# Second norm's scale and shift on z's turned tiles instead of on w1, with fewer counting matmuls, another border and a last tile in halves

## The reference, cut to what matters

```python
xn = _layernorm(x, axis=-1)                       # x is 1250 x 1024
x = x + _L0_gnn_ref(xn, ...) + _L0_mix_ref(xn)    # 20000 edges, attention over them
x = x + _L0_ffn_ref(_layernorm(x))                # gate, up, down with rounded operands

def _L0_gnn_ref(x, W, a, src, dst):
    h = x @ W
    e = exp(-leaky_relu((h @ a_l)[src] + (h @ a_r)[dst], 0.1))
    rowsum = segment_sum(e, src, N)
    return elu(segment_sum(e[:, None] * h[dst], src, N) / (rowsum[:, None] + EPS))

def _L0_mix_ref(x, ...):
    x2 = _layer_norm(x, ln1_g, ln1_b)
    ...                                           # linear attention, cos and sin features
    x = x + (attn @ wo + bo)
    x2 = _layer_norm(x, ln2_g, ln2_b)             # the second norm, g2 and b2
    h = relu(x2 @ w1 + b1)                        # w1 is 1024 x 512
    return x + (h @ w2 + b2)
```

## Time and profile before

| | us |
|---|---|
| runs | 1209.41, 1206.21, 1209.04 |
| median of the runs | 1209.04 |
| the profiled execution, its own time | 1210.66 |
| its span | 1208.4 |
| PE busy | 1154.3 |
| DVE busy | 744.5 |
| ACT busy | 705.4 |
| POOL busy | 326.6 |

### The profile page before, as it was taken

The page is one execution under the profiler, slowest core; times in us unless marked ns, Lnnn a source line. Parts: engine busy times, 40 slices in busy tenths (PEclk is TensorE's granted clock), DMA queues, the critical chain, the costliest instruction groups (busy, mean ns, idle before and its releaser), DMA issues. The chain is left out here.

```text
span 1208.4 us, 19464 instructions
## 1 busy us (share of the span) xinstructions
PE 1154.3 (96%) x6733; PEld 1015.9 (84%) x6733; DVE 744.5 (62%) x1289; ACT 705.4 (58%) x1080; POOL 326.6 (27%) x295
## 2 busy tenths in 40 slices
PE   5999899999999999999899999999989999999997
PEld 2456699999999999999878778999968888887784
DVE  7888636656565565656774777777763222655656
ACT  8497267778777878777875433233344432554553
POOL 1300033333332324232122110666624331211100
PEclk9999999999999999999999999999997999999999
DMA  8000130202020202020537568233353323512103
GB/s 228 16 27 27 39 88 2 73 0 73 0 73 0 73 0 73 0 73 0 195 122 229 152 187 217 54 86 90 79 190 102 103 69 124 187 34 69 35 2 101
DMA packets 73736, 99.43 MB, mean 82 GB/s; under 512 B 27532, under 2 KB 54956, under 8 KB 73172
## 3 DMA queue, kind: packets, MB, share of 16 engines
q1 hardware_dynamic: 70224, 86.11, 25.3%
q0 software_dynamic: 3456, 12.58, 3.5%
HBM read 77.04 MB, written 21.63 MB: 82 GB/s over the span
## 5 line engine op out<-in xcount | busy, mean ns | idle before, releaser
L1149 POOL TENSOR_TENSOR cos_sin_lo<-cos_sin,cos_sin_hi 125x1024 fp32r<-125x1024 f32 (+1 forms) x40 | 95.6, 2391 | 225.3 <-ACT cos_sin_hi L1261 225.3
L1652 PE MATMUL rows_in_psum<-x,mix_hi_q 128*128 128x416 f32 (+1 forms) x384 | 104.0, 352 | 0.0
L1652 PE MATMUL rows_in_psum<-x,mix_hi_k 128*128 128x416 f32 (+1 forms) x376 | 102.8, 355 | 0.0
L850 PE MATMUL rows_in_psum<-h_hi,a_lo 125*125 125x342 f32 x300 | 96.4, 321 | 5.3 <-POOL a_lo L686 3.0
L1756 PE MATMUL rows_in_psum<-x,xt_hi 128*125 128x512 f32 x320 | 100.4, 395 | 0.0
L561 PE MATMUL rows_in_psum<-hot_s,hot_k 125*125 125x314 bf16 x396 | 87.5, 323 | 9.4 <-DVE hot_k L470 8.6
L850 PE MATMUL rows_in_psum<-h_lo,a_hi 125*125 125x342 f32 x300 | 95.7, 319 | 0.0
L850 PE MATMUL rows_in_psum<-h_hi,a_hi 125*125 125x342 f32 x300 | 95.7, 319 | 0.0
L1652 PE MATMUL rows_in_psum<-x,mix_hi_v 128*128 128x416 f32 (+1 forms) x336 | 91.3, 353 | 0.0
L1261 ACT ACTIVATE cos_sin_hi<-cos_sin 125x1024 fp32r<-125x1024 f32 (+1 forms) x80 | 83.6, 1045 | 7.3 <-PE rows_in_psum L1734 5.5
L561 PEld LDWEIGHTS rows_in_psum<-hot_s,hot_k 125*125 125x125 bf16 x396 | 41.5, 137 | 53.5 <-DVE hot_k L470 53.3
(11 more groups left out here) (342 smaller groups left out, 3115.4 us busy)
## 6 DMA issues: line engine op xcount, KB each, us to landing
x_in<-in_x_dram SPq DMA_DIRECT2D x31, 448.0 KB
attn_dram<-attn_t SPq DMA_DIRECT2D x8, 625.0 KB, 4.0
at_in<-attn_dram SPq DMA_DIRECT2D x10, 500.0 KB, 4.6
x_in<-gnn_dram SPq DMA_DIRECT2D x10, 448.0 KB
out_dram<-rows SPq DMA_DIRECT2D x10, 448.0 KB
mix_in_v<-in_L_mix_wv_dram SPq DMA_DIRECT2D x8, 512.0 KB, 6.1
mix_in_k<-in_L_mix_wk_dram SPq DMA_DIRECT2D x8, 512.0 KB, 4.8
mix_in_q<-in_L_mix_wq_dram SPq DMA_DIRECT2D x8, 512.0 KB, 6.9
```

The source lines that it names most:

```text
L850: last = pe.matmul(p_o[0:T, i % 2, n, 0:H_COLS], stationary(left, i, d), right[:, d, cols], start=(d == 0 and m == 0), stop=(d == NT - 1 a ...
L1149: pool.tensor_tensor(full(cs_lo, k), full(cs, k), f32(full(cs_hi, k)), ALU.subtract).then_inc(s_cslo[0], 1)
L1652: last = pe.matmul(p_w[:, n, 0:w], left[which][:, k, :], right[:, k, a:a + w], start=(k == 0 and m == 0), stop=(k == K8 - 1 and m == 2))
```

## The change

Five edits come together.

- Counting: the matmuls of zeros that opened a window are gone; the first chunk's matmuls start the banks instead, and the last chunk's end the first bank. One closing matmul of 2 columns is left. The first chunk stands ahead of the loop and the last two behind it, on PE and on VectorE.
- Border: SP's store of gnn tile 8 and its load of x(0) move from the end of the attention to the start of the project stage, in the other order, ahead of bo; the last addition of b2 moves from GpSimd to VectorE.
- Project stage: the 32 products of b2 with w1, and VectorE's addition behind them, are gone; w1 is split unscaled. z0's and z1's turned tiles are scaled and shifted by ScalarE out of PSUM, in eight pieces, and then copied.
- Feed forward: the same for z2 to z9 in keep_zt. The transposes wait for the scaled copy (s_zt), not for the lower half; normalise(i) waits for the lower half.
- Last tile: result(9) and its store come in two halves of 512 columns; PE signals s_d after each half of down(9). keep_hidden(8), ScalarE's copy of the turned hidden tile 8, waits for down(6) and no longer for down(7).

```diff
@@ counting, PE (VectorE likewise)
-                    for n, (a, w) in enumerate(BANK_PIECES):
-                        pe.matmul(p_cnt[0:T, t % TURNS, n, 0:w], zeros[:], zero_rows[:, 0:w], start=True, stop=False)
...
+                    def chunk(count, slot, start=False, stop=False):
+                        pe.wait_ge(s_hot, count)
+                        for n, (a, w) in enumerate(BANK_PIECES):
+                            last = pe.matmul(p_cnt[0:T, t % TURNS, n, 0:w], hot_k[:, slot, 0:T], hot_s[:, slot, a:a + w], start=start,
+                                             stop=(stop and n == 0))
+                        last.then_inc(s_used, 1)
...
+                    chunk(pe.snap(done, min_val=0, max_val=DONE_MOST) + 1, 0, start=True)
+                    with pe.Fori(first + HOT, past, HOT):
+                        before = pe.snap(done, min_val=0, max_val=DONE_MOST)
                         for j in range(HOT):
...
+                            chunk(before + j + 2, (j + 1) % HOT)
                         pe.reg_add(done, done, HOT)
-                    for n, (a, w) in enumerate(BANK_PIECES):
-                        last = pe.matmul(p_cnt[0:T, t % TURNS, n, 0:w], zeros[:], zero_rows[:, 0:w], start=False, stop=True)
-                    last.then_inc(s_tile, 1)
+                    before = pe.snap(done, min_val=0, max_val=DONE_MOST)
+                    for j in range(1, HOT):
+                        chunk(before + j + 1, j, stop=(j == HOT - 1))
+                    pe.reg_add(done, done, HOT)
+                    pe.matmul(p_cnt[0:T, t % TURNS, 1, 0:2], zeros[:], zero_rows[:, 0:2], start=False, stop=True).then_inc(s_tile, 1)
@@ border
-                if i < NT - 1:
+                if i < NT - 2:
                     store(i)
                     core.load_x(sp, (i + 2) % NT, i % 2)
...
-            add_b2(NT - 1)
-            pool.wait_ge(s_xb, NT)
+            pool.wait_ge(s_xb, NT - 1)
...
+            core.wait_x(dve, NT - 1, 1)
+            dve.tensor_tensor(x_in[:, 1, :], x_in[:, 1, :], b2[:], ALU.add).then_inc(s_xb, 1)
...
+            core.load_x(sp, 0, 0)
+            core.move(sp, core.gnn_dram[NT - 2], core.attended[:, 0, :], core.gnn_stored[0])
             core.move(sp, bo, spread(inp["L0_mix_bo"], T), s_bo)
@@ project stage
-                act.activation(core.w1_hi[:, k, :], w1_raw(k), ACT.Copy, scale=g2[:, k:k + 1]).then_inc(s_whi, 1)
+                act.activation(core.w1_hi[:, k, :], w1_raw(k), ACT.Copy).then_inc(s_whi, 1)
...
-                dve.scalar_tensor_tensor(core.w1_lo[:, k, :], w1_raw(k), g2[:, k:k + 1], f32(core.w1_hi[:, k, :]), ALU.mult,
-                                         ALU.subtract).then_inc(s_wlo, 1)
+                dve.tensor_tensor(core.w1_lo[:, k, :], w1_raw(k), f32(core.w1_hi[:, k, :]), ALU.subtract).then_inc(s_wlo, 1)
...
-            for f in range(F4):
-                for k in range(K8):
-                    last = pe.matmul(p_c[:, f:f + 1], w1_raw(k)[:, f * 128:(f + 1) * 128], b2c[:, k:k + 1], start=(k == 0),
-                                     stop=(k == K8 - 1))
-            last.then_inc(s_c, 1)
@@ feed forward, keep_zt on ScalarE
                 act.wait_ge(s_t, i + 1 - KEPT)
+                for k in range(K8):
+                    last = act.activation(zt(i)[:, k, :], p_t[:, k // 4, (k % 4) * T:(k % 4 + 1) * T], ACT.Identity,
+                                          scale=g2[:, k:k + 1], bias=b2c[:, k:k + 1])
+                last.then_inc(s_zt, 1)
                 act.wait_ge(s_1, F4 * (i // 2))
...
+                act.activation(zt_hi[:, :, (i % 2) * T:(i % 2 + 1) * T], zt(i), ACT.Copy).then_inc(s_thi, 1)
...
-                act.activation(hid[:, f, :], p_1[:, f % 2, 0:2 * T], ACT.Relu, bias=core.c1[:, f:f + 1]).then_inc(s_h, 1)
+                act.activation(hid[:, f, :], p_1[:, f % 2, 0:2 * T], ACT.Relu, bias=b1c[:, f:f + 1]).then_inc(s_h, 1)
...
-                    act.wait_ge(s_d, 2 * (i // 2))
...
+                    act.wait_ge(s_d, i - 1 if i >= NT - 2 else 2 * (i // 2))
...
-                pe.wait_ge(s_tlo, min(NT, 2 * (i // 2) + 6) - KEPT)
+                pe.wait_ge(s_zt, min(NT, 2 * (i // 2) + 6) - KEPT)
@@ last tile, PE and VectorE
+                    if n == 1 or i == NT - 1:
+                        last.then_inc(s_d, 1)
...
+            for n in range(2):
+                dve.wait_ge(s_d, NT + n)
+                half = rows[:, NT - 1, n * 512:(n + 1) * 512]
+                dve.scalar_tensor_tensor(half, down_at(NT - 1)[0:T, n, :], factor[:, NT - 1, 2:3], half, ALU.mult, ALU.add).then_inc(s_out, 1)
```

98 lines of the change are left out of this document (50 added, 48 removed).

## The result

The changed kernel takes 1211.31 us in the median of 19 runs (1210.02 to 1212.85), the kernel before 1209.04 us (19 runs, 1206.21 to 1211.31). The ratio is 1.0023 (95% interval 1.0017 to 1.0030): a little slower, 0.2%. The profiled execution took 1211.54 us, its span 1209.5.

What follows compares the result with a forecast made beforehand. PE was taken as the bound, busy 1154.3 of 1208.4 us. The terms -4.3 - 4.0 + 11.9 - 2.3 = +1.3 on a median of 1209.04 gave 1210.3 us, with an 8-in-10 range of 1204.2 to 1215.6.

Steps and rivals of the forecast that it cites:

- Same: Whole kernel: a time between 1205.4 and 1212.7 us, within 0.3% of the kernel before; chance 0.52.
- Counting: Counting stage: 80 zero matmuls removed and 20 short ones added save 4.3 us, ends 2.5 and 6.
- windows 2 to 11 gain next to nothing: Counting: ScalarE sets the pace in the ten windows that also carry the second norm, so they hardly gain.
- rival B: Counting: windows thought ScalarE-paced are paced by PE, gain 8.8 instead of 4.3 us, total 1205.8; chance 0.08.
- 0.41 for each of windows 12 to 19: Counting: each of these eight windows gains 0.27 us plus half of the closing pair, 3.3 in sum.
- low end: Counting: gain of only 2.5 us if the peeled loop's added branches take it back in eight windows.
- Border and products: Attention's end and project stage: shorter border and dropped w1 products together save 4.0 us, ends 2.5 and 6.
- Feed forward: Feed forward: eight activations in keep_zt make results late and PE wait, costing 11.9 us, ends 7 and 14.
- rival C: Feed forward: TensorE's clock falls in each of rounds 1 to 3, 4.5 us on top, total 1214.8; chance 0.15.
- Last tile: Tail: 1.1 us from PE's wait, 0.5 from VectorE's half, 0.7 from the smaller store, 2.3 us saved.
- Rival D: Project stage: products(2) starts no earlier, gains shrink from 4.0 to 1.0 us, total 1213.3; chance 0.14.
- A: Feed forward: delays overlap and a round waits once, costing 7 instead of 11.9 us, total 1205.4; chance 0.12.

Runs made afterwards that it cites:

- e_add_on_dve: Kernel before with one edit: the last addition of b2 runs on VectorE behind its last sum, not on GpSimd; 1207.59 us, ratio 0.9993.
- e_counts_closing: Kernel before with one edit: a counting window's two closing matmuls have 2 columns instead of 314 and 311; 1205.80 us, ratio 0.9979.
- e_ff_no_scale: Changed kernel with the feed forward's keep_zt as before, leaving out scale and shift of tiles 2 to 9; 1199.22 us, ratio 0.9927.
- e_ff_one_scale: Changed kernel with one activation of 1000 columns for the eight of 125 in the feed forward's keep_zt, values partly wrong; 1199.19 us, ratio 0.9919.
- e_ff_round_x_later: Changed kernel with keep_zt(2c+3) ahead of round_x(2c-1) in ScalarE's order of the feed forward; 1206.72 us, ratio 0.9988.
- e_border_undone: Changed kernel with the border as before: SP's store and load at the attention's end, GpSimd's last b2 addition; 1211.58 us, ratio 1.0028.
- e_counts_undone: Changed kernel with the counting as before: zeros at both ends of a window, no peeled loop; 1216.65 us, ratio 1.0071.
- e_all_but_scale: Changed kernel with scale and shift back on w1 and the bias, with the 32 products; counting, border and last tile stay; 1202.03 us, ratio 0.9945.

## Why the prediction was right, and where it was not

Forecast 1210.3 in 1204.2 to 1215.6, measured 1211.3; a sum of +1.3 against +1.1 in the profiles and +2.3 in the medians. "Same" had 0.52, and the measured 0.23% is inside 0.3%. By its steps:

1. Counting: -4.3 worked out, -4.7 measured. The step "windows 2 to 11 gain next to nothing" failed (1.55): it took one window without a wait for all ten, of which seven had one, so a part of rival B came true. So did 0.41 for each of windows 12 to 19 (0.27): the two pairs do give that much there (0.27 and 0.10 to 0.14), and the peeled loop, which the step had left to its low end, takes 0.12 of it. The two errors cancel.
2. Border and products: -4.0 worked out, -5.2 in the profiles. Every wait named in the step is there (gap 1.4, part 6 2.2, idle before products(2) 8.3, half clock behind it), and z0's and z1's eight activations cost nothing, as it said: from products(3) to the stage's end it is 81.2 us in both. What failed is the base: the step took VectorE's 3.38 us, and the low clock at the stage's start, for fixed, and neither is. Over e_add_on_dve's and e_counts_closing's profiles the gain is 0.1 to 0.2. The blocking of the two engines was right; that 0.06 us decide which one pays was to be seen in the earlier trace rows, and I passed over it.
3. Feed forward: +11.9 worked out, +13.1 measured: rounds 0 and 1 4.9 against 6.5, of which 1.7 is the clock's fall (rival C, one of the three falls it had), rounds 2 and 3 3.5 each against 3.4 and 3.3. PE's waits in the rounds grew by 10.4, near the 12 that the step asked for. The mechanism is shown by e_ff_no_scale, e_ff_one_scale and e_ff_round_x_later together.
4. Last tile: -2.3 worked out, -1.1 measured. The 1.1 for PE's gap was right (1.03), the 1.2 for the halves was not (0.1): the 0.5 from VectorE came (0.4), but the step left out the two DMAs more that SP issues one after the other, and the 0.7 for half of the bytes did not come.
5. Rival D's mechanism (products(2) starts no earlier) did not come; A's neither: the waits of a round do add up.

That the total came out so close is luck. Against the working, the spans have -0.4 in the counting, -1.2 at border and products, +1.2 in the feed forward, +1.2 at the end and -1.1 in the middle, which together leave -0.2. And the 5.2 of border and products is one over a profile that lay 1.6 us over its median: beside an execution like e_add_on_dve's the same sum would have come out near +6, while the medians have +2.3.

## What to carry to other kernels

When a step is moved off an idle-looking engine's path, follow the queue it stands in: ScalarE was 58% busy and had room for 23 us more, yet 2.9 us more for each of eight tiles cost PE 13, because the order was fixed and its slack was 1.4 us; 45% of the added time cost a tenth of that, and an exchange of two lines gave 4.5 of it back. Before a gain is booked on a wait in one profile, look whether a tie decides it: two engines whose additions start 0.06 us apart can come in the other order, and the profile shows one of the two. Look also whether the profiled execution lies near the median. Work dropped from the bounding engine is worth only what its successor can start sooner: 11.4 us of products were worth about 1 us or 4 to 5, depending on what held the next ones up.

## What the runs showed of the hardware

- A VectorE addition with both inputs in SBUF took 1.23 us when it started first and 3.38 when GpSimd's had started 0.06 us before, when GpSimd's had started first it took 2.37, when VectorE's had, 2.99 and 3.31: the one that comes first runs, and the other's time contains it.
- Eight single-precision matmuls of 512 columns took 7.03 us at a granted clock of 1.00, the same product as 32 of one column 10.6 to 11.4 us, with the clock at 0.81 to 0.85 in the first 4 us and 0.50 after, though PE was never idle by its records.
- The same idle time ended either way. After an idle PE of 1.92 us the clock fell to 0.58 for 3.3 us in the changed kernel and did not in e_border_undone, with the same instructions there. After one of 2.4 us, at the start of the project stage, it was 0.53 for 3.2 us in e_border_undone and 1.00 in e_add_on_dve, whose timelines are alike there:

Stretches, e_border_undone (length, busy us of each engine, PEclk, DMA share, GB/s):

```profile
880.80:884.00 3.20, 3.16 (x8) 2.44 (x9) 2.24 (x2) 3.20 (x4) 0.00 (x0) 0.53 0.71 239
```

Stretches, e_add_on_dve (length, busy us of each engine, PEclk, DMA share, GB/s):

```profile
886.30:889.00 2.70, 2.05 (x8) 1.44 (x9) 1.73 (x2) 2.70 (x3) 0.00 (x0) 1.00 0.72 240
```

Behind PE's idle 2.4 us at the end of the counting the clock fell in ten of the fourteen kernels profiled (0.57 to 0.68 in the next 4 us) and stayed at 1.00 in four. Behind the idle 1.59 us ahead of the feed forward it fell in none, but behind one of 1.74 us in e_counts_undone it did:

Timeline of PE, then a stretch, e_counts_undone:

```profile
896.75 0.75 PE L2132 MATMUL rows_in_psum<-wo_rest,at_lo 128*125 128x512 f32 x2 [1.74 <-DVE wo_rest L122]
...
896.80:900.80 4.00, 4.00 (x12) 3.14 (x13) 2.69 (x4) 1.20 (x2) 0.00 (x0) 0.68 0.91 336
```

Not tried: the kernel before with the new counting, keep_hidden's earlier wait and the addition on VectorE, but SP's DMAs in their old place. By the stages above (144.5 + 585.9 + 278.5 + 174.9 + 13.6) it would have a span of about 1197.4, an estimate, and a low one, since the 278.5 comes from an execution 2.0 us under its median. The lowest median of a kernel that computes everything is e_all_but_scale's, 1202.03.
